# The places of three groups of indirect scatters in GpSimd's order are spread, so that one attention group's mask stands after every four of them

## The reference, cut to what matters

```python
x = x + 0.5 * ffn(layernorm(x), weights)      # layer 1
x = x + dilated_attention(layernorm(x))       # layer 2
x = x + 0.5 * ffn(layernorm(x), weights)      # layer 3, the same weights

def ffn(x, ...):
    ...                                       # q, k, v; 16 heads of 8 numbers
    scores = where(causal, q @ k.T / sqrt(8), lowest)
    o = (softmax(scores) @ v) @ w_o
    h = layernorm(x + o, g1, b1)
    probs = softmax(h @ wg)                   # 8 experts
    topv, topi = top_k(probs, 2)              # two experts for each row
    ...
    h1 = gelu(h @ w1[e] + bb1[e])             # 128 -> 512
    y = h1 @ w2[e] + bb2[e]                   # 512 -> 128
    return layernorm(h + sum of w * y, g2, b2)
```

## Time and profile before

| what | value |
|---|---|
| timed runs, median (lowest to highest) | 1053.31 us (1052.3 to 1055.62) |
| the profiled execution, its span | 1192.8 us |
| PE busy | 1022.4 us, 86% |
| DVE busy | 680.8 us, 57% |
| ACT busy | 670.5 us, 56% |
| POOL busy | 572.7 us, 48% |
| mean granted PE clock | 0.898 of full speed |
| indirect scatters (line 1222) | 128, mean 972 ns |
| selects (line 1173) | 256, mean 721 ns |

### The profile page before, as it was taken

One profiled execution on the slowest core, in us unless ns is written; L12 is line 12 of the kernel. 1 busy time (PEld: TensorE's weight loads), 2 busy tenths in 40 slices (PEclk: granted clock), 3 DMA queues, 4 the chain that ended last, 5 costly groups with the idle time before them and its releaser, 6 DMA issues. The chain is left out here.

```text
span 1192.8 us, 29724 instructions
## 1 busy us (share of the span) xinstructions
PE 1022.4 (86%) x10913; PEld 818.6 (69%) x10913; DVE 680.8 (57%) x2458; ACT 670.5 (56%) x1494; POOL 572.7 (48%) x693
## 2 busy tenths in 40 slices
PE   4799979998989989999989989998999988866470
PEld 2566656886877867686777867687777866766470
DVE  5657665655558835686568835686556723520314
ACT  1243424875758756675667757576666756534240
POOL 2223356235465455555565455554464456542515
PEclk9988877998999989898999979799999979887795
DMA  3394105555555545555556545555556545676562
GB/s 71 86 193 109 37 19 162 167 164 181 154 160 150 172 138 156 147 154 172 149 154 171 165 137 144 153 158 154 160 163 176 170 137 164 202 244 221 212 194 51
DMA packets 117239, 181.01 MB, mean 152 GB/s; under 512 B 13128, under 2 KB 80232, under 8 KB 117096
## 3 DMA queue, kind: packets, MB, share of 16 engines
q1 hardware_dynamic: 108904, 162.32, 47.7%
q0 software_dynamic: 8192, 16.79, 4.9%
HBM read 145.10 MB, written 38.68 MB: 154 GB/s over the span
## 5 line engine op out<-in xcount | busy, mean ns | idle before, releaser
L1173 POOL TENSOR_SCALAR_AFFINE_SELECT probs<-probs 128x512 f32<-128x512 f32 x256 | 182.5, 721 | 262.1 <-ACT probs L706 257.1
L706 ACT ACTIVATE probs<-ps_quad 128x768 f32<-128x768 f32 x256 | 193.7, 807 | 150.3 <-PE ps_quad L527 87.8
L744 ACT ACTIVATE act<-ps_ring,weights 128x128 f32<-128x128 f32 x696 | 191.8, 387 | 96.4 <-PE ps_ring L623 48.0
L874 DVE TENSOR_REDUCE shift_cols<-ps_quad 128x2 f32<-128x512 f32 (+3 forms) x256 | 149.9, 586 | 139.8 <-PE ps_quad L508 125.6
L632 PE MATMUL ps_ring<-weights,act 128*128 128x128 f32 x1392 | 190.8, 285 | 31.1 <-issue 16.4
L632 PEld LDWEIGHTS ps_ring<-weights,act 128*128 128x128 f32 x1392 | 174.5, 198 | 35.1 <-issue 21.6
L623 PE MATMUL ps_ring<-tile_t,weights 128*128 128x128 f32 x1392 | 187.6, 292 | 3.9 <-issue 3.2
L623 PEld LDWEIGHTS ps_ring<-tile_t,weights 128*128 128x128 f32 x1392 | 174.0, 204 | 16.8 <-issue 13.2
L1236 POOL DMA_INDIRECT picked<-sorted_outputs,place x128 | 123.7, 966 | 79.8 <-issue 78.6
L999 DVE TENSOR_TENSOR tile_y<-ps_ring,weights 128x128 f32<-128x128 f32 x174 | 48.8, 287 | 182.2 <-PE ps_ring L632 101.2
L1222 POOL DMA_INDIRECT sorted_rows<-h_rows,place x128 | 124.5, 972 | 53.5 <-issue 34.6
(11 more groups left out here) (165 smaller groups left out, 1531.5 us busy)
## 6 DMA issues: line engine op xcount, KB each, us to landing
weights<-expert_weights SPq DMA_DIRECT2D x174, 578.0 KB
tile_rows<-sorted_rows SPq DMA_DIRECT2D x56, 192.0 KB
sorted_outputs<-tile_y SPq DMA_DIRECT2D x56, 192.0 KB
query_key_parts<-qk SPq DMA_DIRECT2D x32, 256.0 KB, 5.0
k<-query_key_parts SPq DMA_DIRECT2D x64, 64.0 KB
q<-query_key_parts SPq DMA_DIRECT2D x64, 64.0 KB
sorted_rows<-zeros SPq DMA_DIRECT2D x2, 1472.0 KB, 10.7
xs<-in_L_attn_x SPq DMA_DIRECT2D x32, 64.0 KB, 2.3
```

Of the source, the lines that this page charges most:

```text
L706: sc.activation(probs[:, r % PROBS, 2 * a:2 * a + 2, :], ps_quad[:, 2 * a:2 * a + 2, 0:3 * P], ACT.Exp, scale=HD ** -0.5).then_inc(pair_fr ...
L744: ins = sc.activation(act[:, k % ACTS, f, :], bank(use)[:, f * P:(f + 1) * P], ACT.Gelu_apprx_tanh, bias=weights_of(k)[:, 2 * F + f:2 * F ...
L874: dve.tensor_reduce(shift_cols[:, late, groups], ps_quad[:, groups, 0:split], AX.X, ALU.max)
L1173: pool.affine_select(out=both, in_=both, compare_op=ALU.is_ge, fill=0.0, base=0, pattern=[[0, 2], [0, 2], [1, P]], channel_multiplier=-1). ...
```

## The change

Three numbers of the table of places are changed.

```diff
-    "turn_mid": 6.856, "route": 7.124, "gate": 7.191, "rank": 11.86, "scatter0": 11.876, "scatter1": 11.917,
-    "scatter2": 12.578, "scatter3": 13.235, "load_tiles0": 13.754, ...
+    "turn_mid": 6.856, "route": 7.124, "gate": 7.191, "rank": 11.86, "scatter0": 11.876, "scatter1": 12.45,
+    "scatter2": 13.0, "scatter3": 13.5, "load_tiles0": 13.754, ...
```

## The result

| kernel | times, median (lowest to highest) | span of the profiled execution | granted PE clock |
|---|---|---|---|
| before | 1052.8 us (1047.11 to 1055.62, four) | 1192.8 us | 0.898 |
| changed | 1059.32 us (1058.0 to 1062.76, four) | 1056.2 us | 0.939 |

The medians lie 6.5 us apart, where 0.7 was forecast. The ratio, which isn't formed from the medians, is 1.0092 with an interval of 1.0049 to 1.0134; that would be 9.7 us. So the change makes the kernel slower by 5 to 14 us. The bigger surprise is the span. The changed kernel's profiled execution spans 1056.2 us and took 1058.0 us by the clock that makes the timed runs, 1.8 us more; recording it cost nothing. So a recording doesn't cost 139.5 us by itself; whether it does for the order of the kernel before is asked next.

The account below looks back on a forecast made before the run. The prediction took PE to bound the kernel and summed its terms for the metric as 0 + 0 + 0.7 + 0 = +0.7 us on 1053.3, so 1054.0 us. The range was 1039 to 1062 us.

Parts of the forecast that it names:

- What bounds the kernel: Whole kernel: PE is the bound, busy 86% of the span, with an undisturbed pace of 12.1 matmuls a us.
- Is the stall in the metric?: Stall behind the eight scatters: mostly the profiled execution's own, which loses 140 us that a timed one does not.
- (a): Eight scatters cut to four and four: profiled span falls to about 1141 us, gain in the metric taken as 0.
- Rival 5: Scatters: stall follows DMA count in some 15 us, so only moves; span near 1193, metric 1054 us; within forecast's 0.46.
- (b): Selects of `exps 10 0`, `10 1`, `10 2` come 5.1 us of POOL issue earlier; nobody gains, cost and gain 0.
- (c): Last four scatters ahead of POOL's `residual`, root and selects of `exps 10 3`: 0 in six sets, 0.7 us in set 0.
- (d): SP's first load of sorted rows goes later, at about 320.6 us; `turn_tiles` on PE has 4.3 us left: cost 0.
- the signs that I gave for (d): New profile: load of sorted rows waits for a scatter in each set; PE's turning of the tiles doesn't wait for it.
- Rival 4: Late landing of scatters: the load overruns its 4.3 us by 1 us in seven sets, 7 us, 1060 us; chance 0.06.
- 1: Stall behind the eight scatters is partly in the timed runs: 12 us less, 1041 us; chance 0.26.
- 2: Stall behind the eight scatters is in the timed runs in full: 34 us less, 1019 us; chance 0.06.
- 3: Last scatter group holds up POOL's selects of `exps X 3`: 10.5 us slower over seven sets, 1064 us; chance 0.16.

Follow-up runs that it names:

- b_again: The kernel before with no edit, profiled once more against itself: ratio 1.0035, 1054.77 us, span 1056.6 us.
- x1_cut_only: Kernel before with the row of eight scatters moved one place later (groups 4, 8, 4), last group not late: ratio 1.0020, 1052.62 us.
- x4_filler: Kernel before with scatters kept early and five added POOL powers ahead of `residual` in sets 0 to 6: ratio 1.013, 1065.13 us.
- x5_load_late: Kernel before with SP's first load of sorted rows also waiting for the selects of `exps X 3`, sets 0 to 6: ratio 1.0024.
- x6_filler_mid: Kernel before with five added POOL powers ahead of `residual` in sets 1 to 5 only: ratio 1.0008.
- x8_early: Kernel before with the last scatters moved earlier, ahead of the selects of `exps X 1` (groups 8 and 8): ratio 1.0057.
- cut_only_2: x1_cut_only unchanged, run again on chip 15, without stalls, against the kernel before: ratio 1.0011.
- late_only_2: x2_late_only unchanged, run again on chip 15, without stalls, against the kernel before: ratio 1.0053.
- x2_late_only: Kernel before with only the last four scatters moved behind the selects of `exps X 2`: ratio 1.0071, 1058.94 us.
- late_mid_2: Kernel before with the last scatter group late in sets 1 to 5 only, on chip 15, without stalls: ratio 1.0050.
- x5b_load_later: Kernel before with SP's first load of sorted rows waiting longer, for DVE's `mid_norm_apply`; no scatter or POOL instruction moved: ratio 1.0212, 1075.04 us.
- late_ends_2: Kernel before with the last scatter group late in sets 0 and 6 only, on chip 15, without stalls: ratio 1.0003.
- x9_late_mid: Kernel before with the last scatter group late in sets 1 to 5 only, on chip 1, with stalls: ratio 1.0054.

## Why the prediction was wrong, point by point

**What bounds the kernel.** Right that PE is the bound; the steady step of 113.8 us is the same in b_again, x1_cut_only, x4_filler, x5_load_late, x6_filler_mid and x8_early.

**Is the stall in the metric?** The answer "not here" was right, the reason wrong. I put the 139.5 us on the recording. In each later execution the time is 1.7 to 1.8 us above the span (1058.0 and 1056.2; 1203.18 and 1201.4 on chip 1), with stalls and without. So the recorded execution took some 1195 us, as on chips 1 and 14, and the three timed runs were of the other kind; on which chips they ran isn't on record. The Trainium skill, "Runtime: NRT & Kernel Launch", launch sequence, says that the profile's total is longer than the reported time by a constant, about 6 us. These traces confirm a constant but neither its size nor its sign: here the span is the shorter, by 1.7 to 1.8 us. The constant should have told me that the profile and the times didn't belong together.

**(a)** In the metric 0, and on chips without stalls x1_cut_only's 1.0020 and cut_only_2's 1.0011 fit that, though they move the row of eight and don't cut it. For the stalled execution I forecast 1141 us from 1192.8; the changed kernel took 1197.22 against 1198.92 us on chip 1 and 1181.17 against 1184.82 on chip 14. So the 52 us were 2 to 4, and neither is clear of noise. The step that failed was to count the hole behind the row of eight as gained time: the hole went, and the time was lost behind the four groups of four. Rival 5, that the stall only moves, was the nearest.

**(b)** Nobody gains from earlier selects: right but for set 0, where PE's `weigh 6 2` waits 2.00 us for them in x1_cut_only and 1.25 in b_again, and not at all in the changed kernel:

```profile
189.68 1.08 PE L540 MATMUL ps_ring<-probs,values 128*32 128x256 f32 x8 [2.00 <-POOL probs L1173]
```

And I looked only at who gains; with the last group behind these selects, POOL's idle time ahead of them, which I quoted, is added to the scatters' delay.

**(c)** Right in sets 1 to 5 (x6_filler_mid 1.0008); set 6 alone wasn't run. In set 0 I counted 0.7 us. The changed kernel's `weigh 6 3`, beside the earlier trace rows, waits 2.75 us for the late selects:

```profile
193.72 1.08 PE L540 MATMUL ps_ring<-probs,values 128*32 128x256 f32 x8 [2.75 <-POOL probs L1173]
```

Less the wait at `weigh 6 2` that went, that is 0.75 us beside x1_cut_only and 1.5 beside b_again. The number came out about right, but by a gain in (b) that I hadn't seen, so by luck.

**(d)** This is the step that made the prediction wrong. I counted 8.6 us of delay as free because `turn_tiles` had 4.3 us left, and named the store and the `spread` behind the load on SP as going "at 322 us or later anyway". Both readings came from the stalled execution, where the wait for the scatters stands only once in SP's list of waits (6.9 us); in b_again it stands eight times (26.8 us in total), so it is what the load waits for in each set. What I said of `turn_tiles` held: PE waits for the load only once in the changed kernel, in the last set, for 7.9 us, and in b_again for 7.5. So the signs that I gave for (d) came true and the step was wrong all the same. It named the store as harmless and went no further; behind the store stood POOL's gathers. Measured: late_only_2 1.0053, x2_late_only 1.0071, late_mid_2 1.0050, that is 5 to 7.5 us, and the changed kernel 1.0092, whose interval takes these in. A cost beyond the late group isn't shown. In the sum, (d) was the term put at 0, and it measured 5 to 7.5 us. Rival 4 had the place (the landing) and, by luck, the size (7 us), but not the consumer: it let PE wait for the load. The Trainium skill, "DMA: Bandwidth & Descriptors", Rules for kernel authors, says to issue a DMA early and wait late. x5b_load_later bears it out: 2.1% for a load 5.6 to 8.6 us later in sets 1 to 5; x5_load_late's 2.3 to 5.3 us cost nothing that can be told from 0.

**The other rivals.** 1 and 2: refuted on chips without stalls. 3: refuted in the middle sets (x6_filler_mid). At the ends the filler costs 9 us, and there it is added work: in set 0 PE waits for selects twice, 2.00 and 4.14 us. The late group, which is moved work, waits once and costs nothing there that can be measured (late_ends_2, 1.0003).

## What to carry to other kernels

Ask of a profile first whether its span fits the timed runs; where it doesn't, no margin read from it holds, since a stall elsewhere makes waits look covered that aren't. A transfer moved back in one engine's list is to be followed through the queue of the engine that waits for it, with each entry behind that wait: here the store, the fifth entry behind the load, was the path, and not PE's use of the load. And idle time of the engine that issues is part of the delay when it stands ahead of the issue.

## What the runs showed of the hardware

The same program takes 1052 to 1054 us in the median on two chips and 1185 to 1199 on two others. On the latter, groups and rows of indirect DMAs on GpSimd are followed by waits of ACT for a releaser that the profile can't name, up to 10.7 us in the sets with attention and 16.2 us in a row of sixteen gathers near the end (x9_late_mid), and PE is granted less clock: 0.88 to 0.93 in the mean of an execution, for 0.93 to 0.96 on the other two. The order of a few scatters has another price on each kind: 4, 8, 4 costs nothing that can be measured on the first and 1.6% on the second, and 4, 4, 4, 4 with a late last group costs 0.9% (0.5 to 1.3) on the first and nothing that can be measured on the second.
